# Attention on one core: the eight queries with most keys as single exponentials on ScalarE, the rest in narrower chunks

## What is computed

```
Q = (x @ Wq + bq).reshape(b, s, H, C) * inv_sqrt_c        # H = 16, C = 64
K = (x @ Wk + bk).reshape(b, s, H, C)
V = (x @ Wv + bv).reshape(b, s, H, C)
scores = jnp.einsum('bshq,bshk->bshqk', Q, K)             # an outer product: q * k
scores = jnp.where(triu(ones((C, C)), 1), -inf, scores)   # query i sees keys 0..i
w = jax.nn.softmax(scores, axis=-1)
attn = jnp.einsum('bshqk,bshk->bshq', w, V)
```

## Time and profile before

| what | value |
|---|---|
| runs, median (lowest to highest) | 3769.89 us (3768.71 to 3771.07), 2 runs |
| the profiled execution, its own time | 3769.08 us |
| its span from first to last instruction | 3767.3 us |
| start of the attention stage (first xT load) | 896.3 us |
| mean granted TensorE clock | 0.973 |
| busy in the span: PE, PEld (weight loads) | 93%, 81% |
| DVE, ACT, POOL | 86%, 48%, 88% |

### The profile page before, as it was taken

One profiled execution on the slowest core, in us unless ns is written; L12 is line 12 of the kernel. 1 busy time (PEld: TensorE's weight loads), 2 busy tenths in 40 slices (PEclk: granted clock), 3 DMA queues, 4 the chain that ended last, 5 costly groups with the idle time before them and its releaser, 6 DMA issues.

```text
span 3767.3 us, 72478 instructions
## 1 busy us (share of the span) xinstructions
PE 3493.9 (93%) x25868; PEld 3070.0 (81%) x26061; DVE 3233.5 (86%) x3516; ACT 1808.7 (48%) x2391; POOL 3307.3 (88%) x1507
## 2 busy tenths in 40 slices
PE   3684999977999999999999999999999999999999
PEld 2342988866888888888888888888888888888888
DVE  8422777666999999999999999999999999999998
ACT  1110443444555555555555555555555555555554
POOL 1677555524999999999999999999999999999998
PEclk7797999998999999999999999999999999999999
DMA  9523566684000000000000000000000000000000
GB/s 377 180 102 110 179 205 204 211 315 165 4 5 5 5 7 5 5 8 5 5 6 6 5 5 5 5 5 5 5 5 6 7 5 8 5 5 6 5 5 5
DMA packets 110620, 209.17 MB, mean 56 GB/s; under 512 B 16609, under 2 KB 77281, under 8 KB 110305
## 3 DMA queue, kind: packets, MB, share of 16 engines
q1 hardware_dynamic: 84192, 140.90, 11.4%
q0 software_dynamic: 21504, 59.93, 4.3%
q10 hardware_dynamic: 4608, 4.20, 0.3%
HBM read 183.34 MB, written 107.74 MB: 77 GB/s over the span
## 4 chain that ended last, share of the span: by engine, by line
POOL 30%; issue 23%; PE 15%; DVE 6%; ACT 1%; another core or an unknown queue 0%; POOLq 0%; DVEq 0%; ACTq 0%
POOL at_s L1303 26%; PE at_num L1550 6%; PE at_den L1550 5%; DVE at_s L1238 3%; PE at_work L1527 2%; DVE at_pv L1238 2%; POOL at_m L1288 2%; PE at_work L1537 1%; POOL at_fall L1285 1%; POOL at_m L1283 1%; PE at_misc L1576 1%; DVE at_k_low L1457 1%; PE at_misc L1582 1%; DVE at_k_top L1454 0%; DVE at_pv L1239 0%
## 5 line engine op out<-in xcount | busy, mean ns | idle before, releaser
L1303 POOL TENSOR_TENSOR at_s<-at_s,at_m 128x2048 f32<-128x2048 f32 (+7 forms) x768 | 2506.5, 3307 | 5.2 <-POOL at_m L1288 4.7
L1389 ACT ACTIVATE at_s<-at_s 128x2048 f32<-128x2048 f32 (+7 forms) x768 | 1085.7, 1419 | 1085.1 <-POOL at_s L1303 1084.5
L1550 PE MATMUL at_num<-k_ident,at_pv 128*128 128x128 f32 (+2 forms) x9216 | 1135.9, 273 | 64.9 <-DVE at_pv L1238 54.5
L1550 PE MATMUL at_den<-k_ident,at_s 128*128 128x128 f32 (+2 forms) x9216 | 1138.6, 273 | 18.2 <-ACT at_s L1389 15.9
L1550 PEld LDWEIGHTS at_num<-k_ident,at_pv 128*128 128x128 f32 (+2 forms) x9216 | 1025.8, 139 | 150.2 <-DVE at_pv L1238 84.1
L1550 PEld LDWEIGHTS at_den<-k_ident,at_s 128*128 128x128 f32 (+2 forms) x9216 | 1029.8, 139 | 55.8 <-ACT at_s L1389 19.1
L1239 DVE TENSOR_TENSOR at_pv<-at_s,at_vp 128x2048 f32<-128x2048 f32 (+7 forms) x512 | 690.2, 1348 | 121.9 <-PE at_num L1550 63.2
L1239 DVE TENSOR_TENSOR at_s<-at_q,at_kp 128x2048 f32<-128x2048 f32 (+7 forms) x512 | 689.4, 1347 | 27.7 <-PE at_den L1550 24.3
L1238 DVE TENSOR_TENSOR at_pv<-at_s,at_vp 128x2048 f32<-128x2048 f32 x256 | 583.9, 2281 | 0.0
L1238 DVE TENSOR_TENSOR at_s<-at_q,at_kp 128x2048 f32<-128x2048 f32 x256 | 581.2, 2270 | 0.0
L706 POOL DMA_INDIRECT picked<-moe_yo,moe_row x256 | 245.8, 960 | 172.0 <-ACT moe_yo L761 84.0
(11 more groups left out here) (248 smaller groups left out, 3007.0 us busy)
## 6 DMA issues: line engine op xcount, KB each, us to landing
c_w<-experts SPq DMA_DIRECT2D x256, 384.0 KB
slot_x<-k_region SPq DMA_DIRECT2D x16, 2144.0 KB, 25.0
moe_x<-slot_x SPq DMA_DIRECT2D x256, 134.0 KB
cmb_y<-picked SPq DMA_DIRECT2D x32, 768.0 KB, 9.1
at_xT<-xT SPq DMA_DIRECT2D x33, 128.0 KB, 2.0
e_x<-u SPq DMA_DIRECT2D x4, 1024.0 KB, 9.7
picked<-moe_yo,moe_row POOLq DMA_INDIRECT x256
xT<-cmb_xT ACTq DMA_DIRECT2D x32, 128.0 KB, 6.2
```

The source lines that it names most:

```text
L1303: nc.gpsimd.tensor_tensor(part(s_slot, c), part(s_slot, c), by_query(m[unit_of(c)][:], c), ALU.subtract).then_inc(sub_done, 1)
L1389: nc.scalar.activation(part(s_slot, c), part(s_slot, c), ACT.Exp, scale=C ** -0.5).then_inc(exp_done, 1)
L1550: ins = nc.tensor.matmul(dst[0:wide, b * P:(b + 1) * P], buf[:, at:at + wide], k.ident[:], start=(c in (0, NTRI) and x == 0 and b == 0), s ...
```

## The change

The far queries 63 to 56 (eight queries, 64 down to 57 keys) leave the chunks. For each of them and each head ACT runs one exponential over all its keys, `exp(k * q/8 + bias)`: q as per-partition scale, minus the row's maximum as per-partition bias, and the sum over keys as third result, into `top_den` (`top_rows`). These are 128 instructions per tile, eight behind each chunk 0 to 15. They read the new key buffer `k_all` with a step of 16 elements and write `top_p` (64 keys x 8 queries x 16 heads) with a step of 128. DVE multiplies `top_p` by v in eight pieces of 1,024 elements (`top_times_v`); PE adds its 64 rows into `num` and `top_den` into `den` (65 transposes). The projection of far queries is made in two parts, QA for the eight (kept by `keep_top`) and the rest; POOL makes the eight queries' maxima apart (`top_maxima`).

The other 24 far queries keep the chunk path, with 384 instead of 512 elements per row. Triangles are cut by a table TRI of (first row, rows), three to five rows a chunk, with a few more elements where a row would not fill a transpose (`margin`); the slot size is 3 instead of 4 rows of 512. Some placements move: SiLU from chunk 18 to 16, the next near q from 19 to 16, the next near V from 22 to 18, the next maxima from 21-23 to 18-20. `out_sb` is gone: the result is added into `x2` in place, and the load of x2 waits for the store before.

```diff
-ROWS = 4
-FULL, TAIL = ROWS * HALF, 64
-TRI_ORDER = ((0, 7, 2, 5, 4, 3, 6, 1), (0, 1, 2, 3, 4, 7, 6, 5))
+TOP = BLK
+SHORT = RANGE - TOP
+REST = SHORT * H
+AW = TOP * H
+TRI = (((0, 3), (27, 5), (3, 3), (22, 5), (6, 3), (17, 5), (9, 4), (13, 4)),
+       ((0, 3), (3, 3), (6, 3), (9, 3), (12, 3), (21, 3), (18, 3), (15, 3)))
+FAR = NTRI + NRECT
+QW = (HALF, REST)
+FULL, TAIL = 3 * HALF, 64
+GROUP = 2
+NGROUP = TOP // GROUP
...
+        def margin(c):
+            left = lambda x: (QW[unit_of(c)] // H - offset(c) - x) % BLK
+            return 0 if is_rect(c) else max([0] + [BLK // 2 - x - left(x) for x in range(lines(c) - 1) if left(x)])
+        def width(c):
+            return (QW[unit_of(c)] // H - offset(c) + margin(c)) * H
...
                 def finish(t):
-                    wait(sp, y_ready, t)
-                    settle(sp, settled)
+                    wait(sp, y_out, 16 * t)
...
+                def top_maxima(t):
+                    pool.wait_ge(scanned, t * 4 + 4)
+                    pool.wait_ge(top_kept, t + 1)
+                    nc.gpsimd.tensor_tensor(rows(top_m), turned(k_top), rows(top_m), ALU.mult).then_inc(top_step, 1)
+                    nc.gpsimd.tensor_tensor(rows(top_fall), turned(k_low), rows(top_fall), ALU.mult).then_inc(top_step, 1)
+                    pool.wait_ge(top_step, t * 3 + 2)
+                    nc.gpsimd.tensor_tensor(top_m[:], top_fall[:], top_m[:], ALU.subtract).then_inc(top_step, 1)
...
-                MAXIMA_HERE, MAXIMA_NEXT = {3: 0, 4: 1, 5: 2}, {21: 0, 22: 1, 23: 2}
-                GATED = 20
+                MAXIMA_HERE, MAXIMA_NEXT = {3: 0, 4: 1, 5: 2}, {18: 0, 19: 1, 20: 2}
+                GATED, TOP_MAXIMA = 18, 21
...
+                nc.gpsimd.memset(top_p[:], 0.0).then_inc(zeroed, 1)
...
+                def top_rows(t, u, low, high):
+                    if low == 0:
+                        act.wait_ge(top_step, t * 3 + 3)
+                        act.wait_ge(k_out, t * 2 + 2)
+                        wait(act, top_summed, t)
+                    for n in range(low, high):
+                        row, head = divmod(n, H)
+                        ins = nc.scalar.activation(view(top_p[:], [[AW, C - row]], row * AW + n),
+                                                   view(k_all[u][:], [[H, C - row]], row * H + head), ACT.Exp,
+                                                   bias=top_m[:, n:n + 1], scale=top_q[:, n:n + 1],
+                                                   accum_out=top_den[:, n:n + 1])
+                        if n % (GROUP * H) == GROUP * H - 1:
+                            ins.then_inc(rows_done, 1)
...
                 def show_v(t, h):
                     act.wait_ge(v_out, t * 2 + (h + 1))
-                    wait(act, pv_done, t * NCH + h * 2 * NTRI)
+                    wait(act, pv_done, t * NCH + h * FAR)
+                    if h:
+                        act.wait_ge(top_pv, t * 2 * NGROUP + NGROUP)
...
-                KEEP_Q1, KEEP_V1, KEEP_Q0, KEEP_V0 = 0, 13, 19, 22
+                KEEP_Q1, KEEP_V1, KEEP_Q0, KEEP_TOP, KEEP_V0 = 0, 13, 16, 17, 18
-                KEEP_UP, SILU = {4: 0, 15: 1, 17: 2}, 18
+                KEEP_UP, SILU = {4: 0, 14: 1, 15: 2}, 16
+                ROWS_AT = [8] * 16
...
+                def top_times_v(t, far, g):
+                    dve.wait_ge(rows_done, t * NGROUP + (g + 1))
+                    at = (0 if far else RANGE) * AW + g * GROUP * H
+                    piece = view(top_p[:], [[AW, RANGE], [H, GROUP], [1, H]], at)
+                    v.tensor_tensor(piece, piece, view(vp[:], [[H, RANGE], [0, GROUP], [1, H]]), ALU.mult
+                                    ).then_inc(top_pv, 1)
...
-                DIVIDE_PAST, DIVIDE_HERE = {5: 0, 6: 1, 7: 2}, {20: 0, 21: 1, 22: 2}
+                DIVIDE_PAST, DIVIDE_HERE = {5: 0, 6: 1, 7: 2}, {17: 0, 18: 1, 19: 2}
+                TOP_V = {7: ((0, 0),), 11: ((0, 1),), 15: ((0, 2),), 18: ((0, 3),),
+                         19: ((1, 0), (1, 1)), 20: ((1, 2), (1, 3))}
...
+                def sum_top_num(t, far):
+                    pe.wait_ge(top_pv, t * 2 * NGROUP + (NGROUP + NGROUP * far))
+                    for key in range(0 if far else RANGE, RANGE if far else C):
+                        ins = nc.tensor.matmul(num[1][:, 0:P], top_p[:, key * AW:(key + 1) * AW], k.ident[:],
+                                               start=False, stop=False, is_transpose=True, skip_group_check=True)
+                    if far:
+                        ins.then_inc(top_summed, 1)
...
-                DOWN_HERE, DOWN_PAST = {20: 0, 21: 1, 22: 2, 23: 3}, {2: 4, 5: 5, 8: 6}
+                DOWN_HERE, DOWN_PAST = {18: 0, 19: 1, 20: 2}, {1: 3, 2: 4, 5: 5, 8: 6}
+                TOP_NUM, TOP_DEN = {18: 0, 21: 1}, 19
```

More of the change, by code:

```diff
@@ L1149, in attention_and_ffn @@
         pv_slot = [a.sb(f"pv{i}", [P, FULL + TAIL]) for i in range(PV_RING)]
[L1150 to L1153, removed]
+        q = [a.sb(f"q{i}", [P, FRONT + QW[i]]) for i in range(2)]
+        m = [a.sb(f"m{i}", [P, FRONT + QW[i]]) for i in range(2)]
+        vv, fall = (a.sb(s, [P, HALF]) for s in ("v", "fall"))
+        k_all = [a.sb(f"k_all{u}", [P, C * H]) for u in range(2)]
+        top_p = a.sb("top_p", [P, C * AW])
+        top_q, top_m, top_fall, top_den = (a.sb(s, [P, AW]) for s in ("top_q", "top_m", "top_fall", "top_den"))
         k_low, k_top = (a.sb(s, [P, H * C]) for s in ("k_low", "k_top"))
@@ L1169, in attention_and_ffn @@
         x2_in, y_out, padded = (a.sem(s) for s in ("x2_in", "y_out", "padded"))
+        top_kept, top_step, rows_done, top_pv, top_summed = (
+            a.sem(s) for s in ("top_kept", "top_step", "rows_done", "top_pv", "top_summed"))
         xT_in = [a.sem(f"xT_in{u}") for u in range(2)]
@@ L1277, in maxima @@
                     n = t * 2 + h
-                    turned = lambda x: view(x[:], [[-1, RANGE], [C, H]], h * RANGE + RANGE - 1)
-                    rows = lambda x, at=0: view(x[:], [[H, RANGE], [1, H]], at)
+                    count_q = QW[h] // H
+                    turned = lambda x: view(x[:], [[-1, count_q], [C, H]], h * RANGE + count_q - 1)
+                    rows = lambda x, at=0: view(x[:], [[H, count_q], [1, H]], at)
                     if step == 0:
@@ L1287, in maxima @@
                         pool.wait_ge(max_step, n * 3 + 2)
-                        nc.gpsimd.tensor_tensor(m[h][:, FRONT:QL], m[h][:, FRONT:QL], fall[:], ALU.subtract
-                                                ).then_inc(max_step, 1)
+                        nc.gpsimd.tensor_tensor(m[h][:, FRONT:FRONT + QW[h]], m[h][:, FRONT:FRONT + QW[h]],
+                                                fall[:, 0:QW[h]], ALU.subtract).then_inc(max_step, 1)
+                def top_maxima(t):
+                    turned = lambda x: view(x[:], [[-1, TOP], [C, H]], C - 1)
+                    rows = lambda x: view(x[:], [[H, TOP], [1, H]])
+                    pool.wait_ge(scanned, t * 4 + 4)
[4 more added lines that the diff above has]
+                    nc.gpsimd.tensor_tensor(top_m[:], top_fall[:], top_m[:], ALU.subtract).then_inc(top_step, 1)
                 def gated(t):
@@ L1327, in keep_k @@
                     wait(act, kp_ready, t * 2 - 1)
-                    for low, dst in ((0, k_near), (RANGE, k_far[u])):
-                        ins = nc.scalar.copy(view(dst[:], [[H, RANGE], [1, HU]], half * HU),
+                    for low, at in ((0, HALF), (RANGE, 0)):
+                        ins = nc.scalar.copy(view(k_all[u][:], [[H, RANGE], [1, HU]], at + half * HU),
                                              view(source[:], [[-1, RANGE], [C, HU]], low + RANGE - 1))
@@ L1498, in tile @@
                             times_v(t - 1, NCH + c - LAG)
+                        for far, g in TOP_V.get(c, ()):
+                            top_times_v(t, far, g)
                         if c in SCAN:
@@ L1640, in _ @@
                 pe.wait_ge(v_out, 1)
-                pe.wait_ge(zeroed, PV_RING + S_RING)
+                pe.wait_ge(zeroed, PV_RING + S_RING + 1)
                 tile_loop(pe, tile)
                 sum_num(NT - 1, NCH - 1)
-                for step in range(4, 7):
+                for step in range(3, 7):
                     down(NT - 1, step)
```

129 lines of the change are left out of this document (80 added, 49 removed).

## The result

The changed kernel takes 4645.65 us (median of two runs, 4645.16 to 4646.15) against 3769.89: 1.2323 times as long, 95% interval 1.227 to 1.2376, 876 us more. The forecast was 4283 in a range of 3800 to 4920: the sign and the mechanism came out, the size was 363 us short.

A forecast was written before the change was run, and what follows sets the result against it. POOL was taken to set the pace before, at 88.65 us a tile. After the change ACT's 26.0 + 27.5 + 51.2 = 104.7 us a tile, 16.05 more, x 32 = 514 us: 3769 + 514 = 4283 us, range 3800 to 4920.

The forecast's parts named there:

- The engines that are relieved: Work per tile on three engines after the change: POOL 73.2 us, DVE 77.8, PE (TensorE) 79.3.
- the side matter: TensorE's clock: at a granted 0.86 its 79 us a tile become 92, under ACT, lengthening only the wait at top_summed.
- The first phase without rows: ACT's other exponentials and copies in a tile until its last new row: 27.5 us.
- The row: One new ACT exponential: 0.40 us, bounds 0.237 to 0.58; 128 rows take 51 us a tile.
- The stride: Part of each ACT row for scattered reads and writes: 0.020 us, between 0 and 0.040.
- the sum: Part of each ACT row for summing over keys: 0.045 us, between 0 and 0.203.
- The stretch: Serial part from a tile's last new row to the next tile's first, ended by TensorE's column sums: 26.0 us.
- rival 1: ACT rows at 0.335 us with stride and sum free: +248 us, 4018 us; chance 0.20.
- rival 2: The sum is a full second ACT instruction, 0.20 us after the first, row 0.555: 4918 us; chance 0.12.
- rival 3: ACT rows start as closely as plain instructions, 0.237 us, break-even 0.275: -155 us, 3615 us; chance 0.10.
- rival 4: Stretch after the rows hidden, tile is ACT's own work: +82, 3851 us; chance 0.13, a third faster, about 3620.
- Signs: Expected in the profile after: ACT near 90% busy, POOL near 70%, ACT's waits on DVE, ACT idle about 13 us a tile.

The follow-up runs named there:

- e_rows4: Changed kernel with 124 of a tile's 128 single exponentials left out, sums filled once: 3585.21 us, ratio 0.9507.
- e_noscale: Changed kernel with a constant scale in the 128 exponentials instead of one number per partition: 4312.97 us.
- e_read1: Changed kernel with the 128 exponentials reading side by side instead of every 16th element: 4432.38 us.
- e_nosum: Changed kernel with the sum over keys left out of the 128 exponentials, sums filled once: 4315.44 us.
- e_plain: Changed kernel with bias, per-partition scale and sum all taken from the 128 exponentials: 3648.88 us.
- Experiment 5: Changed kernel with 62 of 64 top-block transposes left out (4556.86 us), that plus far V first (4460.33), or `keep_top` copies also ahead of SiLU, nothing omitted (4579.87).
- e_write1: Changed kernel with the 128 exponentials writing side by side instead of 128 elements apart: 4647.96 us.
- e_rows64: Changed kernel with every second of the 128 single exponentials left out: 3699.38 us.
- experiment 2: Four kernels, each the changed kernel less the row's sum (4315.44 us), per-partition scale (4312.97), scattered read (4432.38) or scattered write (4647.96).

## Why the prediction was right, and where its size was off

- *The engines that are relieved.* POOL was forecast at 73.2 us a tile; 504.65/800 x 116.1 is 73.2. DVE 77.8, measured 79.1. In e_rows4, at a granted 1.00, all three stand by the same sum as forecast: 72.9, 77.6, and TensorE 79.9 for 79.3. In the changed kernel TensorE has 90.9 at a granted 0.92. That this is near the 92 of the side matter is luck in part: the 92 took a clock of 0.86, and 79.3 at 0.92 would be 86; what the other 5 us are stays open.
- *The first phase without rows*, 27.5 us: the 25 us between the rows, and 2.5 of chunk 0 and q, which the views count in the stretch. Right.
- *The row*, 0.40 us: this term was mis-sized. Of its parts, the start with two operands (0.285) and the elements (0.050) hold: the second operand costs 0.095 by e_noscale. The stride was put at 0.020 and costs 0.05 (e_read1); the sum was put at 0.045, half a shortest instruction, and costs 0.09, a whole one in its distance (e_nosum). 0.285 + 0.050 + 0.050 + 0.090 = 0.475, measured 0.473. I had taken the middle of two bounds twice, and both times too low. For the sum the upper row was the right one, the 0.087 between neighbours. For the stride the upper bound was near by luck: it came from DVE's scattered write, and what ACT pays for is the read, while its write is free. 4,096 x 0.073 = 299 us.
- *The stretch*, 26.0 us: 30.6 - 2.5 = 28.1. It ended as written, with ACT ready and TensorE's sums of the top block last (forecast 1.6 us of waiting, found 2.63). TensorE ended at 30.6 and not 28.6 because it came to V at 10.6 us instead of 8.9. 32 x 2.1 = 67 us. With the row that is 366 of the 363 us by which the forecast fell short.
- *Rivals.* Free stride and sum (rival 1) fell by e_read1 and e_nosum; the sum as a second instruction (rival 2) was right in kind, but it costs 0.09 behind its row and not 0.20, as neighbours overlap. Rows under 0.275 (rival 3) fell; e_plain, with rows at 0.20, shows its break-even from the fast side. A hidden stretch (rival 4) fell: ACT is busy 694.11/800 x 116.1 = 100.7 us a tile and the tile takes 116.1. (Its fast part was priced at about 3620 us; 83 us a tile give 3588.) Experiment 5 moved the stretch's end by 2 to 6 us, so the stretch is on the path.
- *Signs.* ACT was forecast near 90% and is at 87%, POOL near 70% and is at 63%, idle time of ACT about 13 us and it is 14.8, all behind the last row, ended by POOL and then TensorE. One sign did not come: ACT's waits were to be on DVE, and of the 14.8 us only 1.9 are; POOL has 6.8 and TensorE 6.1.

The Trainium skill, Advanced Engine Details and Errata, section SBUF Cachelines, stands against scattered accesses, and by it I had named the upper end of the stride. e_read1 agrees for the reads (0.05 us for some 60 elements, as much again as the elements themselves). For ACT's writes at a step of 128 elements e_write1 shows no price; there the measurement decides.

What stays open: whether a split that gives ACT fewer queries, with the rest back in the chunks, would beat the kernel before. e_rows64 (3699 us) has half the rows, but its other four queries are not computed anywhere; what they cost in the chunks was not tried. Nor was another spread of the 128 rows: all kernels here keep them behind chunks 0 to 15, and rows behind the later chunks, in the stretch where ACT waits 14.8 us, would be an obvious one.

## What to carry to other kernels

A short instruction is priced by the distance of its starts, part by part: here start, operands, readout and scattered read are 0.42 of 0.473 us, and the elements that one wanted to move are 0.05. Work that is moved to an engine with room is hidden only as long as that engine doesn't also carry the hand-offs of the others in its order; count from the last moved instruction to the first of the next round, along every chain. When an edit that shortens a wait changes nothing, look at the wait behind it before the theory is dropped: here the one was worth 0 alone and 3.0 us a tile once the other was gone.

## What was not expected of the hardware

TensorE's clock fell within the stretch. Windows of the kernel after, around TensorE's longest idle time of the tile (columns as in the earlier trace rows, the clock third from the end):

```profile
2040.00:2052.00 12.00, 9.50 (x69) 7.83 (x69) 8.81 (x8) 11.97 (x39) 7.23 (x3) 1.00 0.07 24
2052.00:2058.00 6.00, 1.65 (x12) 1.23 (x11) 2.23 (x3) 5.94 (x8) 0.26 (x1) 0.94 0.00 0
2058.80:2061.20 2.40, 2.40 (x16) 2.40 (x15) 2.03 (x2) 1.79 (x5) 2.40 (x3) 0.61 0.00 0
2062.00:2082.00 20.00, 20.00 (x153) 17.77 (x152) 15.61 (x19) 6.62 (x11) 17.70 (x14) 1.00 0.01 2
2085.00:2125.00 40.00, 28.48 (x183) 24.95 (x183) 28.47 (x22) 39.97 (x135) 26.92 (x10) 0.87 0.00 1
```

TensorE was busy 1.65 of 6 us, waiting for ACT's copies, and the 2.4 us behind that were granted 0.61, most of them at the lower level (1.2 of 2.4 GHz); then it was 1.00 again. TensorE's timeline shows what it did to the same work:

```profile
2050.70 1.47 PE L1636 MATMUL at_num<-k_ident,at_pv 128*128 128x128 f32 x12
...
2057.72 1.22 PE L1612 MATMUL at_work<-k_region,at_xT 128*128 128x128 f32 x4 [3.84 <-ACT at_fall L1384]
...
2058.84 2.38 PE L1636 MATMUL at_num<-k_ident,at_pv 128*128 128x128 f32 x12
...
2062.04 1.88 PE L1612 MATMUL at_work<-k_region,at_xT 128*128 128x512 f32 x4
```

Twelve transposes took 2.38 us instead of 1.47, 0.9 us on the very chain that ends the stretch, and about half of the 1.7 us by which V came late. The side matter of the prediction had the clock as an average over the tile that only lengthens a wait. The average hides where the loss falls. Most of it lies among the rows, as the last of the windows shows (0.87 over 40 us of the next tile): there TensorE was busy 28.5 of 40 us and had time to spare, while ACT worked 39.97 of them. The 0.9 us in the stretch are a small part, but they stand where TensorE is on the path.

The other surprises are the two of experiment 2: an ACT instruction with a sum is two (the readout 193 ns long, 0.09 us in distance), and here ACT pays for a scattered read of SBUF (0.05 us for some 60 elements 16 apart) but not for a scattered write (128 apart).
